# Centring instead of normalising the first two tiles of a gated MoE and BitNet kernel, with the deviation applied after the product

## The reference

```python
for e in range(E):                                    # 4 experts
    g = silu(einsum('bsd,fd->bsf', hidden, Wg[e]))    # Wg = Wu = Wd = ctx_2048
    u = einsum('bsd,fd->bsf', hidden, Wu[e])
    y = einsum('bsf,df->bsd', g * u, Wd[e])
    out = where(expert_ids == e, y, out)
x = x + tanh(g_xattn) * experts(layernorm(x))
x = x + tanh(g_ffn) * bitnet_ffn(layernorm(x))        # ternary weights, 8-bit activations
```

## Time and profile before

| | |
|---|---|
| Median of 3 runs | 421.14 us (420.02 to 422.06) |
| The profiled execution | 422.38 us |
| Its span, from the first to the last instruction | 420.4 us |
| PE busy | 390.6 us (93% of the span) |
| DVE busy | 365.4 us (87%) |
| ACT busy | 291.2 us (69%) |
| POOL busy | 178.7 us (43%) |

### The profile page before, as it was taken

One profiled execution on the slowest core, in us unless ns is written; L12 is line 12 of the kernel. 1 busy time (PEld: TensorE's weight loads), 2 busy tenths in 40 slices (PEclk: granted clock), 3 DMA queues, 4 the chain that ended last, 5 costly groups with the idle time before them and its releaser, 6 DMA issues.

```text
span 420.4 us, 7393 instructions
## 1 busy us (share of the span) xinstructions
PE 390.6 (93%) x2203; PEld 270.0 (64%) x2203; DVE 365.4 (87%) x652; ACT 291.2 (69%) x450; POOL 178.7 (43%) x208
## 2 busy tenths in 40 slices
PE   1899999999999999988999999999999999999891
PEld 0347788888887664755666666666666666667740
DVE  5788587679885889999999999999999999998980
ACT  4446686687784343667878878878878878877960
POOL 0667311014123202174475575575575575522021
PEclk9999999999999999999999999999999999999998
DMA  7759474065000001336255245255155155155241
GB/s 257 251 160 410 157 247 154 1 212 189 2 13 2 0 14 38 39 62 90 50 101 126 49 103 126 46 108 125 42 112 125 38 112 125 39 113 114 50 101 50
DMA packets 48968, 43.66 MB, mean 104 GB/s; under 512 B 42672, under 2 KB 42800, under 8 KB 46896
## 3 DMA queue, kind: packets, MB, share of 16 engines
q1 hardware_dynamic: 44224, 27.11, 23.4%
q0 software_dynamic: 4720, 16.26, 16.3%
HBM read 21.33 MB, written 4.19 MB: 61 GB/s over the span
## 4 chain that ended last, share of the span: by engine, by line
PE 77%; DVE 11%; issue 5%; DMA 4%; ACT 1%; POOL 0%; DVEq 0%; SPq 0%; POOLq 0%; ACTq 0%
PE bank L461 21%; PE bank L584 12%; PE bank L591 11%; PE bank L560 10%; PE bank L567 10%; PE bank L423 9%; DVE prod L1174 2%; DVE mixed L1201 1%; DVE ct_lo L964 1%; DMA xqT<-xq 1%; DMA xs<-x_dram,order 1%; PE bank L528 1%; DVE prod L1201 1%; PE bank L677 1%; DMA yqT<-yq 1%
## 5 line engine op out<-in xcount | busy, mean ns | idle before, releaser
L584 PEld LDWEIGHTS bank<-cst,mT 128*128 128x128 f32 x512 | 66.3, 191 | 14.1 <-issue 2.7
L584 PE MATMUL bank<-cst,mT 128*128 128x128 f32 x512 | 67.8, 276 | 4.0 <-ACT mT L829 4.0
L560 PE MATMUL bank<-wq,xqT 128*128 128x512 bf16 x240 | 61.6, 379 | 1.7 <-DMA xqT<-xq 1.7
L591 PE MATMUL bank<-wq,yqT 128*128 128x512 bf16 x240 | 61.3, 379 | 0.7 <-DMA yqT<-yq 0.7
L567 PE MATMUL bank<-wq,xqT 128*128 128x512 bf16 x240 | 61.6, 379 | 0.0
L829 ACT ACTIVATE mT<-bank 128x512 f32<-128x512 f32 x64 | 37.6, 592 | 18.4 <-PE bank L423 18.4
L406 POOL DMA_INDIRECT out_dram<-res,order x16 | 19.5, 1217 | 70.8 <-DVE res L1295 70.8
L817 ACT ACTIVATE y<-y,yqs 128x512 int8<-128x512 f32 x56 | 40.2, 717 | 9.9 <-POOL yqs L366 9.9
L854 ACT ACTIVATE sg<-bank,gate_s 128x512 f32<-128x512 f32 x60 | 41.0, 683 | 7.4 <-PE bank L560 7.2
L1174 DVE TENSOR_TENSOR prod<-bank,sg 128x512 f32<-128x512 f32 x64 | 43.4, 677 | 1.1 <-ACT sg L854 0.8
L834 ACT ACTIVATE y<-bank 128x512 f32<-128x512 f32 x64 | 37.6, 588 | 8.8 <-PE bank L584 8.6
(11 more groups left out here) (154 smaller groups left out, 810.2 us busy)
## 6 DMA issues: line engine op xcount, KB each, us to landing
mixed<-mixed POOLq DMA_DIRECT2D x15, 512.0 KB, 5.3
stage<-ctx_dram SPq DMA_DIRECT2D x4, 1024.0 KB, 7.5
stage<-wgate_dram SPq DMA_DIRECT2D x4, 1024.0 KB, 8.5
stage<-wup_dram SPq DMA_DIRECT2D x4, 1024.0 KB, 4.7
stage<-wdown_dram SPq DMA_DIRECT2D x4, 1024.0 KB, 4.7
yqT<-yq SPq DMA_TRANSPOSE x60, 2.4
cst<-consts_dram SPq DMA_DIRECT2D x1, 274.0 KB, 3.3
xs<-x_dram,order POOLq DMA_INDIRECT x16, 4.2
```

The source lines that it names most:

```text
L560: last = nc.tensor.matmul(ps_gate[:, :], xqT[:, b, c, :], wq[:, 0, c * F + 512 * n:c * F + 512 * (n + 1)], start=(c == 0), stop=(c == DC - 1))
L584: last = nc.tensor.matmul(bank_[:, c * P:(c + 1) * P], mT[:, n % 2, c, :], had, start=True, stop=True)
L591: last = nc.tensor.matmul(ps_down[b][:, :], yqT[:, m, g, :], wq[:, 2, block_ * D:(block_ + 1) * D], start=(m == 0 and g == 0), stop=(m == ...
```

## The change

The first two tiles are no longer normalised before the product but only centred (`centre`), so that their transposes do not wait for POOL's deviation. Since the product is linear, the reciprocal deviation, now kept in `first_rstd`, is applied to its result: as the scale of the Silu and as a scalar factor in the DVE's multiplication. `first_product` waits for the arrival of the context matrix (`ctx_in`, raised by a nop on ACT) instead of for its rounded copy. `ct_upper(3)` goes behind the first Silu. The spins become 20 and 3, with no wait between. On the DVE, `stats(2)`, `act_mul(0)` and `normalise(2)` go ahead of `ct_lower(1)`.

```diff
+        first_rstd = sb("first_rstd", [P, 2], F32)
...
+        ctx_in = sem("ctx_in")
...
-                nc.gpsimd.tensor_tensor(item_rstd[:, b:b + 1], item_var[:, b:b + 1], neg_half[:, :],
+                rstd = first_rstd if k < FIRST else item_rstd
+                nc.gpsimd.tensor_tensor(rstd[:, b:b + 1], item_var[:, b:b + 1], neg_half[:, :],
                                         ALU.pow).then_inc(rstd_set, 1)
...
             def first_product(k, between=None):
                 e = expert_of(k)
-                pe.wait_ge(ct_hi_set, e + 1)
+                pe.wait_ge(ctx_in, e + 1)
...
-            spin(18)
-            pe.wait_ge(stats_set, 1)
-            spin(5)
+            spin(20)
             x_transposes(0, 0)
-            spin(4)
+            spin(3)
...
             def silu_h(k):
                 act_e.wait_ge(h_done, k + 1)
-                nc.scalar.activation(sil, (first_h[k] if k < FIRST else ps_h)[:, :], ACT.Silu).then_inc(sil_set, 1)
+                if k < FIRST:
+                    act_e.wait_ge(rstd_set, k + 1)
+                    nc.scalar.activation(sil, first_h[k][:, :], ACT.Silu,
+                                         scale=first_rstd[:, k:k + 1]).then_inc(sil_set, 1)
+                else:
+                    nc.scalar.activation(sil, ps_h[:, :], ACT.Silu).then_inc(sil_set, 1)
...
+            def ctx_arrived(e):
+                act_e.wait_ge(in_slot[e], 16)
+                nc.scalar.nop().then_inc(ctx_in, 1)
+
             for e in range(E - 1):
+                ctx_arrived(e)
                 ct_upper(e)
             x_upper(0, 0)
             x_upper(1, 1)
+            ctx_arrived(E - 1)
+            silu_h(0)
             ct_upper(E - 1)
-            silu_h(0)
             a_upper(0)
...
+            def centre(k, b):
+                dve.wait_ge(stats_set, k + 1)
+                ts(xn[:, b, :], rows(k), item_mv[:, b, 0:1], None, ALU.subtract).then_inc(xn_set, 1)
...
             def act_mul(k):
                 dve.wait_ge(sil_set, k + 1)
-                tt(act, (first_h[k] if k < FIRST else ps_h)[:, :], sil, ALU.mult).then_inc(act_set, 1)
+                if k < FIRST:
+                    stt(act, first_h[k][:, :], first_rstd[:, k:k + 1], sil, ALU.mult, ALU.mult).then_inc(act_set, 1)
+                else:
+                    tt(act, ps_h[:, :], sil, ALU.mult).then_inc(act_set, 1)
...
             dve.wait_ge(gathered[0], 16)
             stats(0, 0, st)
+            centre(0, 0)
             dve.wait_ge(gathered[1], 16)
             stats(1, 1, st)
-            normalise(0, 0)
-            normalise(1, 1)
+            centre(1, 1)
             ct_lower(0)
+            dve.wait_ge(gathered[2], 16)
+            dve.wait_ge(rstd_set, 1)
+            stats(2, 0, st)
+            act_mul(0)
+            normalise(2, 0)
             ct_lower(1)
-            act_mul(0)
-            dve.wait_ge(gathered[2], 16)
-            stats(2, 0, st)
             a_lower(0)
-            normalise(2, 0)
             dve.wait_ge(gathered[3], 16)
+            dve.wait_ge(rstd_set, 2)
             stats(3, 1, st)
             act_mul(1)
             x_lower(2, 0)
```

## The result

The changed kernel takes **422.16 us** (median of 20 runs, 421.48 to 423.63), the kernel before 421.02 on the same chip (20 runs, 419.91 to 422.35). The ratio is 1.0027 [1.0017, 1.0037]: 1.14 us slower, within the 0.5% bound. The profiled execution of the changed kernel took 423.63 us, its span 421.7 with a mean granted clock of 0.985; before, 422.38, 420.4 and 0.996.

The account below looks back on a forecast made before the run. The prediction took the DVE and its order of work as the bound in this stage. A DVE delay of 2.05 less 0.59 given back made 1.46, rounded to 1.5 us, on 421.14: 422.6 us, range 421.0 to 424.2.

Parts of the forecast that it names:

- The forecast step: On the DVE, normalise(2) waits for POOL until 27.2, so a_lower(1) ends at 38.75, 2.05 us later; forecast's chance 0.36.
- the 25.2: Start of normalise(2) if nothing on POOL is held: 420.6 us in all, chance 0.06.
- Given back: At item 3, TensorE no longer waits through ScalarE for a weight transfer: 0.59 us comes back, bounds 0 and 0.59.
- Hidden edits: The Silu's scale operand and act_mul(0)'s second multiplication are hidden by the DVE's wait, up to 3 us.
- The break-even at 25.15: The start of normalise(2) on the DVE from which downward the front's gain decides.
- The front: TensorE's first transposes start at about 16.6 instead of 18.39, a gain of 1.8 us; first Silu at 22.25.
- The power is not held: POOL's second power runs free under ct_lower(0): normalise(2) at 26.5, 421.9 us in all, chance 0.16.
- The clock: TensorE's clock falls in its waits before down_product(0): 0.7 us more, 423.3 to 423.9, chance 0.12.
- the prediction's own signs: Forecast wrong if normalise(2) starts before 25.15 or the granted clock drops below 2.4 GHz between 27 and 36.
- Costing the spins at nothing: The PE spins, 18, 5 and 4 becoming 20 and 3, lie in TensorE's wait and cost nothing.
- The sum: Whole kernel: 2.05 − 0.59 = 1.46, rounded to 1.5 us later, 422.6 from a median of 421.14.

Follow-up runs that it names:

- Experiment 1: The changed kernel with POOL's item_scale(2) ahead of gathers 3 to 6: 419.16 us, ratio 0.9954 to the kernel before.
- experiment 2: The changed kernel with the DVE's order of before put back, centring kept: 421.49 us, ratio 1.0004 to the kernel before.
- experiment 4: The changed kernel with ct_upper(3) back in front of the first Silu: 422.56 us, ratio 1.0028 to the kernel before.
- experiment 6: The changed kernel with 4 and 9 more spins in TensorE's two later waits: 423.5 and 422.88 us (1.0044, 1.0045 of before), 423.02 in one profile.
- experiment 7: The changed kernel unaltered: 422.46 us, 1.0041 of before; with 4, 9 and 2 spins and a wait before the first transposes: 422.94, 1.0057.
- experiment 3: The changed kernel with ct_lower(0) behind the statistics of tile 2 on the DVE: 422.21 us, ratio 1.0021 to the kernel before.
- experiment 8: Changed kernel, item_scale(2) ahead of gathers 3 to 6, plus ct_lower(3) behind a_lower(1): 421.48 us, 1.0007 of before; plus front wait and 2 spins instead: 419.24, 0.9956.

## Why the prediction was right, and where its terms were off

**The forecast step, right.** The gain of the front went into a wait for POOL's `item_rstd`: `normalise(2)` at 27.21 for 27.2 predicted, the power held (2.48), and from there 11.51 to the end of `a_lower(1)`, 38.72 for 38.75. Experiment 1 removed the wait and the sign turned; experiment 2 removed the order behind it, and the loss shrank: in the median to 0.04%, in the stage from 2.0 to 0.7 at `update(0)`. The 2.0 in the stage was measured in six executions (experiments 4, 6 and 7), those in which the clock was not low for long there. The Trainium skill, SBUF — State Buffer, section "Who interferes with whom", had the power held by a DVE instruction with two inputs in SBUF, and 2.48 agrees. Its exception for descriptor generation does not: gather 3 took 3.12 in experiment 3 and 2.60 in experiment 2, against 1.01 free. The prediction also misread what follows from the section: with the power held, `ct_lower(0)` is over before gather 3, so its two sentences together give the 27.2 of the forecast, and the 25.2 needs the power free as well.

**Given back, right.** 0.59 at item 3, by the mechanism named: no transfer wait on ScalarE, 1.01 instead of 1.60. The second execution profiled (experiment 7) gives back 0.61 there as well.

**Hidden edits, right.** ScalarE's split is worth nothing here (experiment 4). The break-even at 25.15 fits experiment 1 (22.84, faster) and the change (27.21, slower).

**The front, mis-sized and harmless.** First transposes at 17.11 for 16.6, first Silu at 22.81 for 22.3: the gather of tile 0 landed 0.6 later in this execution (its statistics start at 15.61, not 15.03). The wait behind it took it all.

**"The power is not held", wrong in the change, its price right.** I put `normalise(2)` at 26.5 for it, with gather 3 held in the power's place. Experiment 3 has that, with `ct_lower(0)` 0.89 later (19.20 for 18.31): 26.5 and 0.89 are 27.39, and 27.36 was measured.

**The clock, the term that failed.** I wrote that it "more likely holds", 0.12 for a fall, from the nearly 5 us without a matmul that it took at the kernel's end. By the mean clocks of experiment 7 it falls in nearly every run, and in the profile shown after idle stretches of 1.10 and 2.35 with 0.66 of transposes between. A stretch below 2.4 GHz between 27 and 36 was one of the prediction's own signs that the forecast is wrong, and it came: the case that happened is the forecast's wait together with the rival's clock. The size of that rival was near: 0.7 predicted, 1.0 for the long fall; the short one costs nothing because TensorE's own waits cover it. Its pace was taken from the kernel's first 11 spins, for which the profile gives a granted clock of 1.00; what shows the pace at 0.50 is the 0.43 between matmuls here. The Trainium skill, TensorE: Matmul & The Clock Gate, section "HAM oscillation — how this bites in real kernels", warned of waits between bursts. The trace agrees that the clock falls, here behind waits of 1.10 and 2.35, shorter than those of the section's example. Costing the spins at nothing was off in the same way: they no longer reach up to the first transposes, and with a gap of 2.09 (experiment 4) or 2.12 (experiment 8) in front of these the clock fell there.

**The sum.** Predicted +1.46. The two comparisons of the changed kernel gave +1.14 and +1.70. The terms in the stage are +2.0, 0 to +1.0 for the clock, −0.6 given back, and a drift of −0.3 that the prediction does not have: +1.1 to +2.1 at the last `update`. That the two medians lie on either side of 1.46 is therefore partly luck: a clock that it had more likely holding and a drift that it did not know partly offset each other. What stays open: the clock's 1.0 is seen in the stage of one execution, but the kernels that hold it (experiments 6 and 7) were not faster in the median. The runs of one kernel can also lie in two groups: of the 30 of before beside experiment 1, 19 lie between 419.9 and 421.3 and 11 between 422.1 and 422.8; of the first 12 of experiment 6, 4 between 421.7 and 422.4 and 8 between 423.3 and 424.4. Whether the transfer near 192 us parts them was not shown. The landing of the first gathers, the transfer near 192 us and the drain differ between executions by as much as the effect; whether the spins also cost something there was not settled.

## What to carry to other kernels

Before moving a step up, look at the in-order queue of the engine that makes its input: here one scalar of the third tile stood behind four gathers on POOL, so the moved step waited and what used to fill the wait was queued behind it. Moving the producer as well turned +0.3% into −0.5%. And a gain that opens a wait on TensorE can be paid for with its clock, so read the granted clock of the stretch, not only the wait.

## What the runs showed of the hardware

POOL was held by the DVE's `ct_lower` (two inputs in SBUF, 2.28) whatever it issued while that ran: the power took 2.48 instead of 0.57, a gather 3.12 instead of 1.01 (experiment 3), the scaling 1.30 instead of 0.19 (experiment 1). A gather issued 0.37 before a `ct_lower` began was not held: 1.10 from 19.20 in the kernel before, where `ct_lower(0)` starts at 19.57. POOL got in between two `ct_lower` that ran back to back: that scaling ended at 30.53, while the pair ran from 28.20 to 32.68.

The granted clock fell to 0.50 behind 1.10 and 2.35 idle around 0.66 of transposes, and stayed low for 6.8 us in one profiled execution of the changed kernel and for 3.4 in the other.

The transposing transfer near 192 us took 4.2 to 4.3 us in two of the 14 profiled executions and 2.4 in the other twelve, which puts 1.6 to 1.7 us of waiting on TensorE or none: as much as this whole change.
